# The second attention stage with the query blocks of its first batch rising and of its last batch falling, and the next batch's keys loaded in other pieces

## The chip, the cores and the metric

The kernel runs on one core of one Trainium2 chip. The metric is the device time of one execution in microseconds (us): 2022.06 before the change, the median of three runs (2018.59 to 2034.35). Lower is better.

## What is computed

Two layers work on `x`, four batches of 1024 tokens by 128 features. Each layer normalises the tokens, runs an attention and a mixture of experts on the result, and adds the product of the two (the experts' output behind a silu) to `x`. The change touches the attention of the second layer alone, which the reference writes as follows:

```
q = (xn @ Wq.T).reshape(B, S, 2 * H, hd).transpose(0, 2, 1, 3) * scaling
k, v = ...
scores = jnp.einsum('bhqd,bhkd->bhqk', q, k)
causal = jnp.triu(jnp.full((S, S), -jnp.inf), 1)
attn = jax.nn.softmax(scores + causal, axis=-1).reshape(B, H, 2, S, S)
w = attn[:, :, 0] - lam * attn[:, :, 1]
o = jnp.einsum('bhqk,bhkd->bhqd', w, v)
o = o * jax.lax.rsqrt(jnp.mean(o * o, axis=-1, keepdims=True) + EPS) * (1.0 - LAMBDA_INIT)
x = x + (o.transpose(0, 2, 1, 3).reshape(B, S, -1) @ Wo.T) * silu(experts(xn))
```

There are 16 score heads of 8 features. The mask is causal, so a block of 128 queries with number b (0 to 7 within its batch) needs only the key blocks 0 to b: b + 1 of them, 36 in a batch, 144 in the stage.

## The kernel before, in words

The program has four stages one behind the other: tokens of layer 0, attention of layer 0, the routed experts, and the attention of layer 1 (`attention_stage(1, ...)`), which is the last.

A unit u of the attention (0 to 31) is one block of 128 queries; units 0 to 7 are the first batch, 8 to 15 the second, and so on. `block_order` says which block a unit takes. Before, in the second layer, every batch goes 0, 7, 1, 6, 2, 5, 3, 4: a short unit and a long one alternate.

A unit goes through these steps. The names are those of the kernel's plan.

- `max`: TensorE makes the scores of the queries against the keys (`row_scores`, L1685, with the mask rows L1661 for the block on the diagonal), and VectorE reduces them to a row maximum (L2039). One reduction takes 1024 columns at most; the blocks 0 to 7 need 2, 4, 6, 10, 10, 12, 14 and 18 of them. Behind the last one of a unit VectorE splits the maxima into three bfloat16 parts (L2045 to L2054).
- `mrow`, `mcopy`, `msplit`: TensorE transposes the maxima (L1952), ScalarE copies them to SBUF (L1901), and a DMA on SP's queue (L1706) writes them as extra rows of the queries, `QS`.
- `exp`: for each key block TensorE makes the scores again, transposed and with the maxima taken off by those extra rows (`far_scores`, L1672), in two halves of 8 heads; ScalarE takes the exponential of each half (L1876). So a key block costs two exponentials of 128x1024.
- `av`: TensorE multiplies with the values (L1975), once for each key block, and gathers in one PSUM bank, `AV`.
- `ocopy`, `oback`, `onorm`: ScalarE copies that bank out (L1890), TensorE transposes it back (L1983), VectorE divides by the sums and prepares the norm (L2061 to L2084). Behind `ocopy` ScalarE also issues the loads of the next batch (below).
- Once for two units: `orms` on GpSimd (L1819 to L1822, the inverse square root), `oturn` and `oproj` on TensorE (L1990, L1995), with `oturned` on ScalarE between them (L1906), `final` on VectorE (L2109) and on GpSimd (L1836), and the store on SP's queue (L1743).
- Beside them the experts' outputs are fetched for two units: gathers on GpSimd (L1766) and a load of x on SP's queue (L1727), and `weigh` (ScalarE, L1855), `mix` (GpSimd, L1774), `tanh` (ScalarE, L1863), `gate` (GpSimd, L1780 and L1782).

Score tiles of `max` and `exp` share three PSUM slots of two banks. `mrow`, `oback`, `oturn` and `oproj` share one bank, `MISC`, which one user holds at a time.

The order on every engine is fixed before the run: `attention_plan` is a list scheduler that takes the steps of all units with costs (`COST`), with an aim for each kind of step in units of u (`AIM`: `max` of u near u - 0.9, `exp` near u + 1.3) and with their dependencies, and writes one list of steps for each engine. The engines run these lists in order and wait for each other through semaphores. In the plan the `mrow` of unit u stands behind the first `exp` of unit u - 2. Both the old and the new block order go through the same scheduler with the same costs and aims.

Keys and values of a batch lie in one of two buffers. The keys of the next batch come in six DMAs: two halves, each in the three runs of `KRUNS` (384, 256 and 128 KB); the values come in one DMA (544 KB in rows of 544 bytes). ScalarE issues them behind the `ocopy` of the units for which `feeds` is true: before, the first half of the keys in the first unit of a batch, the second half in the second, the values in the third (`load_piece`, L608 and L602).

## Time and profile before

| | |
|---|---|
| median of 3 runs | 2022.06 us (2018.59 to 2034.35) |
| the profiled execution | 2009.26 us, span 2007.4 us, so 1.9 us around it |
| mean granted TensorE clock | 0.889 of full speed |
| busy over the span | TensorE 81%, VectorE 66%, ScalarE 58%, GpSimd 55% |
| attention of layer 1 | from 1392.1 us to the end at 2007.4 us |

Times are us from the span's start. In a row of the timeline the first number is the start, the second the time from the start of the first to the end of the last of the merged instructions (xN says how many), then engine, line, operation and the tiles; the bracket says how long the engine had been idle and what ended that. SPq and ACTq are the queues on which SP and ScalarE issue DMAs; the time of a merged row there holds the waits between the issues. A window's row gives, for each engine, busy us and the count of instructions, then the granted clock (1.00 is 2.4 GHz, 0.50 is 1.2 GHz), the share of the DMA engines and GB/s.

### The profile page before, as it was taken

To read this page: it belongs to the slowest core of one execution; us is meant where nothing else is said; L and a number is where in the kernel's file an instruction comes from. 1 tells how busy PE (TensorE), PEld (TensorE's weight loads), DVE (VectorE), ACT (ScalarE), POOL (GpSimd) and SP (SyncE) were. 2 spreads that over 40 slices of the span, in tenths; PEclk is the share of its full clock that TensorE was granted. 3 is DMA by queue.
4 is the path that set the end of the run, shared out by engine and by line. 5 is a ranking of instruction groups with operands and counts; after the bars stand their busy time and mean duration, and the time that the engine had idled before them with its cause. 6 is when DMAs were issued, how large, how long until landed. Compare 5 with 4: busy or idle time off the path is not lost. (4 is left out here: it accounts for less than half of the span.)

```text
span 2007.4 us, 77167 instructions
## 1 busy us (share of the span) xinstructions
PE 1620.5 (81%) x33422; PEld 1255.6 (63%) x33422; DVE 1322.0 (66%) x1921; ACT 1171.6 (58%) x1500; POOL 1098.2 (55%) x1104
## 2 busy tenths in 40 slices
PE   6888789989999999999997633487778778778776
PEld 4666677777787777788785523376445545555554
DVE  5553767778777767768786342255877677677673
ACT  2333477777787777778785321154556556556555
POOL 4755488888899788978986265001222222222211
PEclk9888799999999999999998665698799799788788
DMA  3355023222332233322221172362121121111100
GB/s 96 97 172 141 24 90 92 75 82 77 103 99 55 82 94 97 86 65 66 74 70 56 57 215 82 100 176 75 40 51 29 44 50 28 49 47 27 30 13 10
DMA packets 189005, 151.47 MB, mean 75 GB/s; under 512 B 92163, under 2 KB 178190, under 8 KB 183166
## 3 DMA queue, kind: packets, MB, share of 16 engines
q1 hardware_dynamic: 161526, 103.80, 18.2%
q10 hardware_dynamic: 20088, 27.00, 4.3%
q0 software_dynamic: 7056, 15.74, 2.7%
q8 instruction: 267, 4.37, 0.9%
q14 instruction: 68, 0.56, 0.1%
HBM read 98.91 MB, written 46.79 MB: 73 GB/s over the span
## 5 line engine op out<-in xcount | busy, mean ns | idle before, releaser
L1876 ACT ACTIVATE a_EX<-bank 128x1024 f32<-128x1024 f32 x624 | 615.0, 1027 | 296.9 <-PE bank L1672 233.0
L2015 DVE TENSOR_TENSOR a_PM<-bank,a_PM 128x1024 f32<-128x1024 f32 x336 | 400.6, 1222 | 121.7 <-PE bank L1672 110.1
L1797 POOL TENSOR_TENSOR a_SN<-a_SN,a_MB 128x1024 f32<-128x1024 f32 x176 | 420.8, 2431 | 41.8 <-DMA a_MB<-m_dram 40.6
L2039 DVE TENSOR_REDUCE a_M<-bank 128x2 f32<-128x1024 f32 (+3 forms) x296 | 330.9, 1163 | 111.2 <-PE bank L1685 74.3
L1975 PE MATMUL bank<-a_EX,VV 128*32 128x128 f32 x9984 | 378.8, 294 | 11.1 <-issue 9.2
L1672 PE MATMUL bank<-QS,KS 51*128 51x128 bf16 (+1 forms) x4992 | 248.4, 233 | 95.0 <-DVE a_M L2039 33.0
L1975 PEld LDWEIGHTS bank<-a_EX,VV 128*32 128x32 f32 x9984 | 279.3, 117 | 62.7 <-issue 36.1
L1672 PEld LDWEIGHTS bank<-QS,KS 51*128 51x128 bf16 (+1 forms) x4992 | 163.9, 101 | 191.0 <-DVE a_M L2039 54.0
L1872 ACT ACTIVATE a_SN<-bank 128x1024 f32<-128x1024 f32 x176 | 176.8, 1024 | 61.0 <-PE bank L1651 59.3
L1651 PE MATMUL bank<-QP,rel_t 112*128 112x32 bf16 x5632 | 198.1, 177 | 3.7 <-issue 3.4
L1880 ACT ACTIVATE a_SN<-a_SN 128x1024 f32<-128x1024 f32 x176 | 184.3, 1058 | 22.8 <-POOL a_SN L1797 22.7
L1651 PEld LDWEIGHTS bank<-QP,rel_t 112*128 112x128 bf16 x5632 | 170.4, 96 | 4.7 <-issue 4.5
L1685 PE MATMUL bank<-KS,QS 48*128 48x128 bf16 (+3 forms) x1152 | 123.2, 302 | 41.6 <-DVE a_M L2039 16.7
L1766 POOL DMA_INDIRECT a_XG<-y_dram,KR x64 | 61.9, 967 | 155.8 <-DMA y_dram<-t_Y 130.0
L1672 PE MATMUL bank<-QS,KR 48*128 48x128 bf16 (+1 forms) x2688 | 123.9, 224 | 28.7 <-DVE a_PM L2015 12.8
L1646 PE MATMUL bank<-QN,KS 112*128 112x64 bf16 x2816 | 141.2, 193 | 7.2 <-PEq L710 5.7
L575 POOL COPY QP<-QS 48x1024 bf16<-48x1024 bf16 x64 | 137.4, 2148 | 0.0
L1672 PEld LDWEIGHTS bank<-QS,KR 48*128 48x128 bf16 (+1 forms) x2688 | 79.3, 97 | 73.9 <-DVE a_PM L2015 30.1
L2022 DVE TENSOR_TENSOR a_PM<-a_SN 128x1024 f32<-128x1024 f32 x64 | 97.9, 1530 | 31.6 <-ACT a_SN L1872 25.4
L1646 PEld LDWEIGHTS bank<-QN,KS 112*128 112x128 bf16 x2816 | 106.4, 98 | 12.5 <-issue 10.3
L1975 PE MATMUL bank<-a_SN,VV 128*32 128x128 f32 x2816 | 106.9, 291 | 4.3 <-ACT a_SN L1880 4.2
L1685 PEld LDWEIGHTS bank<-KS,QS 48*128 48x128 bf16 x1152 | 45.0, 100 | 98.6 <-issue 41.9
(213 smaller groups left out, 2286.5 us busy)
## 6 DMA issues: line engine op xcount, KB each, us to landing
a_MB<-m_dram SPq DMA_DIRECT2D x32, 1024.0 KB, 5.3
QS<-q_dram SPq DMA_DIRECT2D x192, 96.0 KB, 3.0
q_dram<-t_PARTS SPq DMA_DIRECT2D x32, 192.0 KB, 3.0
k_dram<-t_PARTS SPq DMA_DIRECT2D x16, 384.0 KB, 3.7
KS<-k_dram ACTq DMA_DIRECT2D x16, 384.0 KB
xs_dram<-bv SPq DMA_DIRECT2D x26, 192.0 KB, 4.8
t_XS<-xs_dram SPq DMA_DIRECT2D x18, 256.0 KB, 4.1
y_dram<-t_Y ACTq DMA_DIRECT2D x18, 256.0 KB, 2.3
```

What stands on the lines that cost most here:

```text
L575: last = pool.tensor_copy(QP[rows, r, :, :, a], QS[rows, q, :, :, :].rearrange("k p h (q b) -> k q (p h) b", b=2)[:, :, :, a])
L1646: pe.matmul(out_b[:, :, 4 * pair:4 * pair + 4], KS[0:KD, it.u // NB % 2, pair, it.jb * P:(it.jb + 1) * P], QN[:, r, pair, q0:q0 + CQ // 2, ...
L1651: last = pe.matmul(out_b[:, i, :], rel_t[:, y:y + P], QP[:, r, q0 + i, :, :].rearrange("k h a -> k (h a)"), start=False, stop=i == CQ // 2 ...
L1672: last = pe.matmul(bank[:, 2 * it.n + hh, k * P:(k + 1) * P], kblock(hh, rows, it.u, it.jb, pair), QS[hh * HALF:hh * HALF + rows, it.u % Q ...
L1685: last = pe.matmul(bank[:, 2 * it.n + hh, k * width:(k + 1) * width], QS[rows, it.u % QR, p0 + k, hh, :], KS[rows, it.u // NB % 2, p0 + k, ...
L1797: pool.tensor_tensor(near_view(sn), near_view(sn), as_near(MB[:, :, :], it.part), ALU.add)\
L1872: act.activation(near_buffer(u, jb)[:, part, :], src.rearrange("p b c -> p (b c)"), ACT.Copy).then_inc(act_done, 1)
L1876: act.activation(as_banks(EX[:, it.need % ER[layer]], part), by_head, ACT.Exp, scale=SCALE).then_inc(act_done, 1)
L1880: act.activation(sn, sn, ACT.Exp, scale=SCALE).then_inc(nexp_done, 1)
L1975: last = pe.matmul(dst_o, VV[:, u // NB % 2, jb, vo:vo + 32], ex, start=bool(it.first) and h < 4, stop=bool(it.last), skip_group_check=True)
L2015: dve.tensor_tensor(pm, mb.rearrange("p hh (k i) -> p hh k i", k=4), pm, ALU.max).then_inc(max_used, 1)
L2039: dve.tensor_reduce(target[:, :, p0:p0 + g], mb[:, :, 0:g * width].rearrange("p hh (k j) -> p hh k j", k=g), AX.X, ALU.max).then_inc(max_u ...
```

## The change

In the second layer the first batch takes its blocks in rising order (0, 1, ... 7) and the last batch in falling order (7, 6, ... 0); the two batches between stay as they were. The loads of the next batch are cut in another way: the first unit of a batch loads run 0 of both key halves (768 KB), the second run 1 of both (512 KB), the third run 2 of both (256 KB), the fourth the values. The first layer is the same as before.

```
-    return k if layer == 0 else (k // 2 if k % 2 == 0 else NB - 1 - k // 2)
+    if layer == 0 or u < NB:
+        return k
+    if u >= UNITS - NB:
+        return NB - 1 - k
+    return k // 2 if k % 2 == 0 else NB - 1 - k // 2
...
 def feeds(layer, u):
-    return u % NB < (5, 3)[layer] and u // NB + 1 < B
+    return u % NB < (5, 4)[layer] and u // NB + 1 < B
...
+        def load_keys(eng, b, k, run, to=KS, src=k_dram):
+            s0, parts = run
+            row = k % 2 * HALF + s0 * DH
+            eng.dma_start(to[row:row + parts * DH, b % 2, :, :].rearrange("r p t -> r (p t)"),
+                          src[b][0:parts, k % 2].rearrange("s d p t -> s d (p t)")).then_inc(kv_in[b % 2], 16)
...
                             if feeds(layer, u):
-                                load_piece(layer, act, u // NB + 1, u % NB)
+                                if layer == 0:
+                                    load_piece(layer, act, u // NB + 1, u % NB)
+                                elif u % NB == len(KRUNS):
+                                    load_piece(layer, act, u // NB + 1, 2)
+                                else:
+                                    for k in range(2):
+                                        load_keys(act, u // NB + 1, k, KRUNS[u % NB])
```

The scheduler makes new lists from this. On ScalarE, the beginning of the stage stood like this before (`a_MP` is `mcopy`, `a_XG` is `weigh`, `a_TH` is `tanh`, `a_EX` is `exp`, `OS` is `ocopy`):

```order
L1901 ACTIVATE a_MP<-bank 48x128
L1855 ACTIVATE a_XG<-a_XG,KR 128x128 x4
L1863 ACTIVATE a_TH<-a_XG 128x256
L1855 ACTIVATE a_XG<-a_XG,KR 128x128 x4
L1863 ACTIVATE a_TH<-a_XG 128x256
L1855 ACTIVATE a_XG<-a_XG,KR 128x128 x4
L1876 ACT_TABLE_LOAD
L1876 ACTIVATE a_EX<-bank 128x2x4x128
L1863 ACTIVATE a_TH<-a_XG 128x256
L1901 ACTIVATE a_MP<-bank 48x128
L1876 ACTIVATE a_EX<-bank 128x2x4x128
L1890 ACTIVATE OS<-bank 128x512
```

In the changed kernel (its lines stand 8 further down, and 14 behind the loads) the same beginning is:

```order
L1915 ACTIVATE a_MP<-bank 48x128
L1863 ACTIVATE a_XG<-a_XG,KR 128x128 x4
L1915 ACTIVATE a_MP<-bank 48x128
L1884 ACT_TABLE_LOAD
L1884 ACTIVATE a_EX<-bank 128x2x4x128 x2
L1871 ACTIVATE a_TH<-a_XG 128x256
L1863 ACTIVATE a_XG<-a_XG,KR 128x128 x4
L1898 ACTIVATE OS<-bank 128x512
L606 DMA KS<-k_dram 24x1x8192 x2
L1871 ACTIVATE a_TH<-a_XG 128x256
L1884 ACTIVATE a_EX<-bank 128x2x4x128 x2
L1863 ACTIVATE a_XG<-a_XG,KR 128x128 x4
```

The exponentials of unit 0 now stand ahead of the first `tanh`, and the `tanh` of the later pairs stand between the exponentials of units 1 and 2.

On TensorE the end of the program stood like this before (`OS` is `oback`, `a_OF` is `oturn`, `wo,a_OT` is `oproj`, `a_EX,VV` is `av`, `QS,KS` is `exp`):

```order
L1672 MATMUL bank<-QS,KS 128x128 x16
L1990 MATMUL bank<-eye,a_OF 128x128 x2
L1975 MATMUL bank<-a_EX,VV 32x128 x16
L1995 MATMUL bank<-wo,a_OT 128x128 x2
L1672 MATMUL bank<-QS,KS 128x128 x16
L1661 MATMUL bank<-mask_b 128x4x64 x4
L1983 MATMUL bank<-eye,OS 128x128 x4
L1672 MATMUL bank<-QS,KS 128x128 x8
L1661 MATMUL bank<-mask_b 128x4x64 x4
L1975 MATMUL bank<-a_EX,VV 32x128 x64
L1983 MATMUL bank<-eye,OS 128x128 x4
L1990 MATMUL bank<-eye,a_OF 128x128 x2
```

In the changed kernel the last rows are:

```order
L1680 MATMUL bank<-QS,KS 128x128 x8
L1669 MATMUL bank<-mask_b 128x4x64 x4
L1989 MATMUL bank<-a_EX,VV 32x128 x32
L1997 MATMUL bank<-eye,OS 128x128 x4
L1989 MATMUL bank<-a_EX,VV 32x128 x48
L2004 MATMUL bank<-eye,a_OF 128x128 x2
L2009 MATMUL bank<-wo,a_OT 128x128 x2
L1997 MATMUL bank<-eye,OS 128x128 x8
L2004 MATMUL bank<-eye,a_OF 128x128 x2
L2009 MATMUL bank<-wo,a_OT 128x128 x2
```

The last score matmuls, which stood between the `oturn` of units 28 and 29 and the `oback` of units 30 and 31, now stand ahead of all of them: `oback` of unit 29, `oturn` and `oproj` of units 28 and 29, and `oback` of units 30 and 31 follow each other with no score between.

## Rows read from the trace of the kernel before

**Rows 1.** Windows: us, busy us of each engine (instructions), granted clock, DMA share, GB/s
```profile
core 0: us, PE busy (x) PEld busy (x) DVE busy (x) ACT busy (x) POOL busy (x), PEclk, DMA share, GB/s
1560.00:1710.00 150.00, 118.78 (x2216) 77.12 (x2212) 108.09 (x168) 84.83 (x113) 41.59 (x92) 0.86 0.16 42
...
1420.00:1500.00 80.00, 65.48 (x1271) 42.91 (x1273) 62.55 (x92) 47.56 (x63) 17.58 (x43) 0.87 0.19 49
```

**Rows 2.** Waits of TensorE from 1560 to 1860: who for whom, us, times, longest
```profile
PE bank L1672 <- DVE a_M L2039: 16.1, 23, 2.2
PE bank L1952 <- DVEq L2055: 8.0, 7, 2.0
PE bank L1685 <- DVE a_M L2039: 6.5, 5, 2.3
```

**Rows 3.** Timeline of ScalarE: first exponential of units 9 and 25
```profile
1573.67 2.16 ACT L1876 ACTIVATE a_EX<-bank 128x1024 f32<-128x1024 f32 x2 [2.46 <-PE bank L1672]
...
1874.93 1.02 ACT L1876 ACTIVATE a_EX<-bank 128x1024 f32<-128x1024 f32 x1 [2.39 <-PE bank L1672]
```

**Rows 4.** Timeline of ScalarE from 1971 to 1990: the last 17 exponentials
```profile
1971.83 2.85 ACT L1876 ACTIVATE a_EX<-bank 128x1024 f32<-128x1024 f32 x3 [0.17 <-PE bank L1672]
...
1975.03 7.48 ACT L1876 ACTIVATE a_EX<-bank 128x1024 f32<-128x1024 f32 x8
...
1982.74 1.18 ACT L1876 ACTIVATE a_EX<-bank 128x1024 f32<-128x1024 f32 x1
...
1984.82 4.68 ACT L1876 ACTIVATE a_EX<-bank 128x1024 f32<-128x1024 f32 x5
```

**Rows 5.** Timeline of VectorE: behind the last reduction of units 1 and 9
```profile
1418.65 0.20 DVE L2045 TENSOR_REDUCE a_MT<-a_M 128x16 f32<-128x48 f32 x1
...
1559.59 0.20 DVE L2045 TENSOR_REDUCE a_MT<-a_M 128x16 f32<-128x48 f32 x1
```

**Rows 6.** Timeline of SP's queue at the start of the stage
```profile
1392.09 14.77 SPq L1727 DMA_DIRECT2D a_XG<-x_mid  x8
1406.91 15.55 SPq L1706 DMA_DIRECT2D QS<-a_MP  x4
```

**Rows 7.** The page's DMA issues: KB each, us to landing
```profile
QS<-q_dram SPq DMA_DIRECT2D x192, 96.0 KB, 3.0
```

**Rows 8.** Timeline of ScalarE at the start: table load and first exponential
```profile
1414.71 1.28 ACT L1876 ACT_TABLE_LOAD   x1
1418.83 1.02 ACT L1876 ACTIVATE a_EX<-bank 128x1024 f32<-128x1024 f32 x1 [2.83 <-issue]
```

**Rows 9.** Timeline of ScalarE at the start: the first two `tanh`
```profile
1403.53 0.42 ACT L1863 ACTIVATE a_TH<-a_XG 128x256 f32<-128x256 f32 x1 [1.69 <-issue]
...
1409.43 0.42 ACT L1863 ACTIVATE a_TH<-a_XG 128x256 f32<-128x256 f32 x1 [3.77 <-POOL a_XG L1774]
```

**Rows 10.** Timeline of TensorE, VectorE and GpSimd at the end
```profile
1984.10 0.41 PE L1990 MATMUL bank<-eye,a_OF 128*128 128x128 f32 x2 [1.14 <-POOL a_OF L1822]
...
1986.86 0.66 PE L1983 MATMUL bank<-eye,OS 128*128 128x128 f32 x4
...
1992.51 0.63 PE L1983 MATMUL bank<-eye,OS 128*128 128x128 f32 x4 [0.81 <-ACT OS L1890]
...
1993.17 0.26 DVE L2061 RECIPROCAL a_RC<-bank 128x16 f32<-128x16 f32 x1 [3.42 <-PE bank L1983]
...
1995.47 0.20 POOL L1819 TENSOR_SCALAR a_SS<-a_SS 128x16 f32<-128x16 f32 x1 [8.00 <-DVEq L2085]
...
2001.29 0.66 PE L1990 MATMUL bank<-eye,a_OF 128*128 128x128 f32 x2 [8.15 <-POOL a_OF L1822]
```

**Rows 11.** Windows with loads of the next batch (first row) and without (second)
```profile
1574.00:1614.00 40.00, 33.32 (x600) 21.87 (x602) 27.28 (x43) 22.66 (x30) 12.22 (x32) 0.83 0.23 58
...
1875.00:1915.00 40.00, 33.24 (x606) 21.65 (x606) 28.19 (x43) 22.93 (x31) 12.58 (x33) 0.84 0.10 26
```

**Rows 12.** The page's 40 slices: GB/s of each
```profile
GB/s 96 97 172 141 24 90 92 75 82 77 103 99 55 82 94 97 86 65 66 74 70 56 57 215 82 100 176 75 40 51 29 44 50 28 49 47 27 30 13 10
```

More of the change, by code:

```diff
@@ L605, in load_piece @@
                 to, src = (KS, k_dram) if k < 2 else (KR, kr_dram)
-                for s0, parts in KRUNS:
-                    row = k % 2 * HALF + s0 * DH
-                    eng.dma_start(to[row:row + parts * DH, b % 2, :, :].rearrange("r p t -> r (p t)"),
-                                  src[b][0:parts, k % 2].rearrange("s d p t -> s d (p t)")).then_inc(kv_in[b % 2], 16)
+                for run in KRUNS:
+                    load_keys(eng, b, k, run, to, src)
         def token_stage(x_src, stage):
```

## The prediction

> **What bounds the kernel now.** I read the windows first. In the steady middle of the second attention stage no engine is full: in the 150 us from 1560 TensorE is busy 118.8, VectorE 108.1, ScalarE 84.8, at a mean clock of 0.86 [rows 1]. So the table of waits comes next: over two batches (300 us) TensorE waits 16.1 + 8.0 + 6.5 = 30.6 us for VectorE's reductions and splits, 15.3 a batch [rows 2], and the rest of its idle time is small gaps between steps. The reader is to see a coupled pipeline: `max` and `exp` share TensorE and three PSUM slots, and each runs slower for the other. Third, the timeline at the two ends, where one of the two streams runs alone.
>
> Three prices follow. **Mixed**: from the first exponential of unit 9 to that of unit 25 two batches pass, 1874.93 - 1573.67 = 301.3 us [rows 3] for 72 key blocks, 4.18 us for one `max` block and one `exp` block together, everything included. **`exp` alone**: the last 17 exponentials run with no `max` beside them, from 1971.83 to 1984.82 + 4.68 = 1989.50, 17.67 us [rows 4], 1.04 each and 2.08 a block. **The share of `max` in the mix** is what is left, 4.18 - 2.08 = 2.10. I treat the mix as additive (so much for each `max` block, so much for each `exp` block); that is the choice on which the sum stands, and the rivals are what happens if it fails.
>
> **The start.** Before, VectorE goes through unit 0 and all 18 reductions of unit 1 (9 blocks), to 1418.65 [rows 5], before the first exponential at 1418.83 [rows 8]. After, unit 1 has two blocks, and by the order on ScalarE the table load and the first exponentials stand behind one `weigh` only. What is late next is SP's queue: eight loads of x stand ahead of the first row of maxima, one behind the other, until 1406.91 [rows 6], and they stay there. The first row then needs its landing; the trace gives none for it, so I take the 3.0 us of the query loads on the same queue [rows 7], which gives 1409.9. The score and mask matmuls and the table load of 1.28 [rows 8], partly beside each other, put the first exponential at an estimated 1412.5, 6.3 us sooner. By then TensorE has issued, in its list, 8 reductions: units 0 and 1 and a third of unit 2, 4 blocks instead of 9, since the remaining ones of unit 2 stand behind the first `exp`. Five more `max` blocks are left for the mix: 5 x 2.10 = 10.5. Net: -6.3 + 10.5 = **+4.2 us**.
>
> The `tanh` of pairs 3, 5 and 7, which lay beside `max` of unit 1, now stand between the exponentials of units 1 and 2. In the trace one `tanh` follows the other by 1409.43 - 1403.53 = 5.9 us [rows 9], because `mix` and `gate` on GpSimd and two gathers lie between them. From 1414.6, behind the first two exponentials, three such steps end at 1432.3, and 0.4 later unit 2's exponentials may start. By the mix, 6 `max` blocks and 3 `exp` blocks from 1412.5 end at 1412.5 + 12.6 + 6.2 = 1431.3. So the chain costs **+1.4 us**; the bounds are 0 and, if all of it stood alone, 1432.7 - 1412.5 - 6.2 = 14.
>
> **The end.** By TensorE's list 20 `exp` steps (10 blocks) stood behind the last `max` step before, and 10 (5 blocks) stand there after. That is no gain by itself: by the additive mix the 5 blocks cost 2.08 each either way. What changes is the tail behind the last exponential. Before: 2007.4 - 1989.50 = 17.9 us. After, the order on TensorE sets a chain with nothing beside it. From the `oback` of unit 29: to the start of `orms` 1995.47 - 1992.51 = 2.96; to `oturn` 2001.29 - 1995.47 = 5.82; `oturn` to the next `oback` 1986.86 - 1984.10 = 2.76; then `oback` and `onorm` of unit 30 and `onorm` of unit 31 (they share VectorE and `MISC`), 2.96 + (1995.47 - 1993.17) = 5.26; `orms` again 5.82; and from `oturn` to the end 2007.4 - 2001.29 = 6.11 [rows 10]. Together 28.7. The `ocopy` ahead of it ends one exponential (1.0) before the last exponential does and hands over in 0.15, so the tail is 28.7 + 0.15 - 1.0 = 27.9 us: **+10.0 us**. Before, the first three of these steps lay beside exponentials of unit 31.
>
> In the falling batch, from unit 26 on, fewer `max` blocks than `exp` blocks run together, so TensorE waits less for VectorE. Of the 15.3 us a batch [rows 2] I take half, **-7.7 us**; the bounds are 0 and all 15.3. In the rising batch I take no such gain, since there the `max` blocks are the larger part. Check: VectorE needs 108.1 / 36 = 3.0 us a block [rows 1], 96 us for the 32 blocks left at 1413; the mix for them and the 21 `exp` blocks of units 0 to 5 is 32 x 2.10 + 21 x 2.08 = 111, so the mix is the larger and stands.
>
> **The loads** stay seven issues and the same bytes for a batch, at the same engine; they are done long before the next batch. A stretch with them and the same stretch of the last batch without them hold the same work: TensorE 33.3 and 33.2 us busy, VectorE 27.3 and 28.2 in 40 us, though the DMA share is 0.23 against 0.10 [rows 11]. I cost them at 0. If the cover went, the small row of maxima would wait for the load issued before it: at the best slice of the page, 215 GB/s [rows 12], 768, 512 and 256 KB in the short units of the start take 3.6 + 2.4 + 1.2 = 7.2 us. The Trainium skill speaks against the change here: "Trainium Kernel Development and Optimization", Key Constraints, says that DMAs issued from the SP, ACT and POOL queues all run on the same 16 engines and interleave. By that rule the sum would be up to those 7.2 us higher; rows 11 don't show it in the middle of the stage, and no row shows it for units as short as those at the start.
>
> **The sum.** 4.2 + 1.4 + 10.0 - 7.7 = +7.9 us. Against the profiled execution: 2009.26 (span 2007.4 and 1.9 around it) becomes 2017.2. That execution lies 12.8 us below the median of the runs and below all three of them, so I carry the difference to the median: 2022.06 + 7.9 = 2030.0 us, 0.4% more. A measurement of this kernel can tell about 1%, 20 us, from no change; the forecast is that it can't be told.
>
> **Rivals.**
>
> *The orders without short-long meetings run better than the mix (faster).* For it: TensorE is busy only 118.8 of 150 us, and 15.3 of the idle time are waits for VectorE. Then VectorE runs the rising batch full: its 32 blocks end at 1413 + 96 = 1509; the 7 `exp` blocks of unit 6 alone take 14 x 1.04 = 14.6; unit 7's 8 beside unit 9 at TensorE's busy time of 118.8 / 36 = 3.3 take 26.4; and with 1573.67 - 1559.59 = 14.1 from the split of unit 9's maxima to its first exponential, as before [rows 3, 5], this comes at 1564.1 instead of 1573.67, -9.6. In the falling batch all 15.3 go, and the tail stays at +10.0: -9.6 - 15.3 + 10.0 = -14.9, which is 2007. The mean clock of 0.86 means that TensorE spends 0.28 of a batch, 42 us, at 1.2 GHz, which would be 21 at 2.4; if the two new batches together won half of one batch's 21, another 10 us would go: 1997. Against it: VectorE has drains and waits for its slots even at the start, when it had nothing else to do.
>
> *VectorE starves in the rising batch (slower).* The place is units 3 to 7, where each `max` step shares three slots with an `exp` step, in a list made by aims that fit the old order. For it: in 1420 to 1500, with the same long units, VectorE is busy 62.55 of 80 us, 78% [rows 1]. At that pace 96 us become 123, `max` of unit 7 ends at 1536, and the first exponential of unit 9 comes at 1536 + 14.6 + 26.4 + 14.1 = 1591, +17.4 instead of +5.6. With no relief in the falling batch and the tail of +10.0: +27.4, 2050. It decides against the forecast once VectorE's busy share there is under 87%.
>
> *The loads collide with the rows of maxima.* +7.2 on the forecast: 2037.
>
> **How the numbers follow.** The forecast has 0.50, the faster rival 0.19, the slower one 0.24, the colliding loads 0.07. The faster rival reaches 20 us only with the clock's help, so 0.11 of it counts as faster by over 1% and 0.08 as within; of the slower one 0.21 is over 1%, and of the forecast and the loads, whose unknown costs spread by some 12 us, 0.09 is over 1% too. That makes faster 0.11, within 1% 0.59, slower 0.30. The range for 8 in 10 goes from 2004, between the faster rival's two ends, to 2053, just past the slower one.
>
> **What would show it.** In the trace after: first exponential near 1412.5 and the loads of x still ahead of the first `msplit`; `tanh` between the exponentials of units 1 and 2, about 6 us apart; VectorE's busy share between 1420 and 1510 (above 87% for the forecast); the first exponential of unit 9 near 1579; the tail from the last exponential near 28 us, with `oturn` of units 28 and 29 waiting for GpSimd. A tail near 18, or unit 9 before 1565, would make the prediction wrong on the fast side; unit 9 after 1590 on the slow side.

## The result, and the profile after

| | before | after |
|---|---|---|
| median (20 runs each) | 2021.85 us (2008.99 to 2034.35) | 2036.96 us (2025.89 to 2047.75) |
| ratio, 95% interval | | 1.0074 (1.0054 to 1.0094) |
| profiled execution, span | 2009.26, 2007.4 | 2036.38, 2034.5 |

The change costs 0.74%, about 15 us. The forecast was 2030.0, within 1%, with a range of 2004 to 2053: the time fell into it, 7 us above the forecast. That a change of this size can't be told from none did not hold: with 20 runs on each side the interval lies clear of 1. The page after begins so:

```profile
span 2034.5 us, 77167 instructions
...
PE 1630.5 (80%) x33422; PEld 1260.9 (62%) x33422; DVE 1314.8 (65%) x1921; ACT 1172.4 (58%) x1500; POOL 1108.3 (54%) x1104
```

The two spans differ by 27.1 us, but not all of that is the change. VectorE's first reduction of the stage, in the timeline before and then after:

```profile
1392.97 2.36 DVE L2039 TENSOR_REDUCE a_MT<-bank 128x8 f32<-128x1024 f32 x2 [1.71 <-PE bank L1661]
```
```profile
1405.72 2.36 DVE L2053 TENSOR_REDUCE a_MT<-bank 128x8 f32<-128x1024 f32 x2 [1.67 <-PE bank L1669]
```

12.7 us lie ahead of the stage, in work that the change doesn't touch. So every profile is read from that reduction on. In ScalarE's timeline after, the first exponentials of units 0, 9, 17 and 21 and the last one of all are:

```profile
1425.17 1.94 ACT L1884 ACTIVATE a_EX<-bank 128x1024 f32<-128x1024 f32 x2
...
1604.02 2.16 ACT L1884 ACTIVATE a_EX<-bank 128x1024 f32<-128x1024 f32 x2 [2.50 <-PE bank L1680]
...
1750.49 2.16 ACT L1884 ACTIVATE a_EX<-bank 128x1024 f32<-128x1024 f32 x2 [2.54 <-PE bank L1680]
...
1828.28 2.15 ACT L1884 ACTIVATE a_EX<-bank 128x1024 f32<-128x1024 f32 x2 [1.16 <-PE bank L1680]
...
2004.78 1.03 ACT L1884 ACTIVATE a_EX<-bank 128x1024 f32<-128x1024 f32 x1
```

Before, units 17 and 21 began here (units 0 and 9 are in [rows 3, 8], the last exponential in [rows 4]):

```profile
1723.67 4.20 ACT L1876 ACTIVATE a_EX<-bank 128x1024 f32<-128x1024 f32 x4 [2.52 <-PE bank L1672]
...
1804.61 2.15 ACT L1876 ACTIVATE a_EX<-bank 128x1024 f32<-128x1024 f32 x2 [1.06 <-PE bank L1672]
```

These cut the stage into four pieces. "First exp" is from the first reduction to the first exponential, "start" from the first reduction to unit 9, "middle" from unit 9 to unit 21, "falling" from there to the end of the last exponential, "tail" the rest. The same for every experiment, in us; each ratio is to the kernel before as it ran beside that experiment, so the time that it stands beside below is not always the same:

| kernel | ratio to before (95%) | first exp | start | middle | falling | tail | stage |
|---|---|---|---|---|---|---|---|
| before | 1 | 25.9 | 180.7 | 230.9 | 184.9 | 17.9 | 614.4 |
| after | 1.0074 (1.0054 to 1.0094) | 19.5 | 198.3 | 224.3 | 177.5 | 28.7 | 628.8 |
| e2_loads | 0.9952 (0.9929 to 0.9975) | 27.0 | 179.0 | 229.2 | 183.8 | 18.0 | 610.0 |
| e3_rise | 1.0091 (1.0054 to 1.0128) | 19.8 | 200.9 | 230.7 | 182.3 | 18.0 | 631.9 |
| e4_fall | 1.0044 (1.0018 to 1.0070) | 26.8 | 182.2 | 232.5 | 178.9 | 28.6 | 622.2 |
| e5_late | 1.0043 (1.0015 to 1.0070) | 19.5 | 190.8 | 225.0 | 174.5 | 28.6 | 618.9 |
| e6_list | 0.9949 (0.9924 to 0.9974) | 24.3 | 175.2 | 224.1 | 181.7 | 18.0 | 599.0 |
| e7_tail | 1.0069 (1.0039 to 1.0099) | 18.6 | 196.4 | 225.1 | 176.8 | 21.0 | 619.3 |
| e8_chain | 1.0120 (1.0101 to 1.0139) | 18.0 | 206.6 | 224.9 | 174.2 | 28.6 | 634.3 |
| e10_chain2 | 1.0075 (1.0049 to 1.0100) | 19.5 | 202.2 | 224.6 | 175.4 | 28.7 | 630.9 |
| e9_best | 0.9933 (0.9912 to 0.9955) | 24.9 | 173.9 | 223.7 | 173.5 | 21.0 | 592.1 |
| e11_split | 1.0085 (1.0054 to 1.0115) | 18.3 | 207.5 | 222.3 | 176.6 | 28.6 | 635.0 |
| e12_bestsplit | 0.9920 (0.9890 to 0.9950) | 23.7 | 175.1 | 224.0 | 176.8 | 20.9 | 596.8 |

The pieces come from one profile each and scatter by some us: the falling parts of kernels with the same falling order lie between 173.5 and 178.9, the starts with the old first batch between 173.9 and 182.2 (in part another list, as the experiments show). The ratios come from many runs.

After against before: +17.6 in the start, -6.6 in the middle, -7.4 in the falling batch, +10.8 in the tail, together +14.4 us, which is what the medians show (15.1). The forecast had +5.6, 0, -7.7 and +10.0.

**The start.** ScalarE's timeline after, from the first exponential of unit 0 to the first of unit 2 (ACTq rows are its DMA issues):

```profile
1423.51 0.27 ACT L1915 ACTIVATE a_MP<-bank 48x128 bf16<-48x128 f32 x1 [8.91 <-PE bank L1966]
...
1442.99 1.92 ACT L1884 ACTIVATE a_EX<-bank 128x1024 f32<-128x1024 f32 x2
...
1448.15 0.60 ACT L1898 ACTIVATE OS<-bank 128x512 f32<-128x512 f32 x1 [0.17 <-issue]
1448.17 1.46 ACTq L606 DMA_DIRECT2D KS<-k_dram  x2
...
1459.62 1.94 ACT L1884 ACTIVATE a_EX<-bank 128x1024 f32<-128x1024 f32 x2 [7.42 <-PE bank L1680]
```

and TensorE's at the same place:

```profile
1450.47 0.61 PE L1693 MATMUL bank<-KS,QS 48*128 48x512 bf16 x2
...
1458.97 1.04 PE L1680 MATMUL bank<-QS,KS 51*128 51x128 bf16 x16 [7.89 <-DMA QS<-a_MP]
```

TensorE stands 7.89 us in front of unit 2's scores, and what ended the wait is the row of maxima of unit 2. It goes out on SP's queue in two DMAs, at 1448.04 and 1448.83, beside the 512 KB that ScalarE put on its own queue from 1448.17 on. The view of the DMA queues from 1448 to 1462 shows these loads (the GB/s are of 40 slices of 0.35 us):

```profile
GB/s 0 0 0 0 18 94 6 0 47 47 47 47 0 47 47 94 48 48 48 48 48 48 50 47 95 48 48 48 48 47 47 94 47 47 47 47 0 0 0 0
...
KS<-k_dram ACTq DMA_DIRECT2D x2, 256.0 KB
QS<-a_MP SPq DMA_DIRECT2D x2, 6.0 KB
```

The two key loads run at some 47 GB/s, not at the 215 of [rows 12], and last from 1449.9 to 1461.0. By the trace's DMA records they go in 32 packets of 16 KB, never more than two at a time, 0.61 us each (median). The row of maxima was issued by 1449.56 and landed at 1458.84, 9.3 us later; rows that meet no load land 1.24 us behind their issue. The records show the waiting packet by packet: the first of the row's two DMAs was through by 1449.56, ahead of the first key packet; of the second one's 24 packets of 256 bytes eight went at once, from 1450.23 to 1450.35, and the other sixteen one by one from 1453.93 to 1457.93, with 16 KB key packets between them. That is the colliding rival of the prediction, in unit 2 instead of spread over three units. By the Trainium skill, "Trainium Kernel Development and Optimization", Key Constraints, DMAs of the SP, ACT and POOL queues share the same 16 engines and interleave; the 9.3 us against 1.24 agree with it, and [rows 11], on which I had set it aside, did not hold for the start.

The waits of TensorE from unit 0's first exponential to unit 9's, after:

```profile
PE bank L1680 <- ACT a_EX L1884: 9.6, 12, 3.8
PE bank L1693 <- ACT a_EX L1884: 8.3, 14, 2.4
PE bank L1680 <- DVE a_M L2053: 8.2, 10, 2.5
PE bank L1680 <- DMA QS<-a_MP: 7.9, 1, 7.9
```

and before (1420 to 1573):

```profile
PE bank L1672 <- ACT a_EX L1876: 3.1, 6, 0.7
...
PE bank L1685 <- ACT a_EX L1876: 2.0, 5, 0.6
```

Beside the new wait for the DMA, TensorE waits 17.9 us for slots that exponentials hold, instead of 5.1. VectorE's busy share in the `max` work of the first batch is 91.91 / 121.20 = 76% (from the windows after), against 78.90 / 106.00 = 74% before:

```profile
1425.20:1546.40 121.20, 83.34 (x1307) 50.05 (x1305) 91.91 (x126) 54.62 (x80) 34.70 (x63) 0.77 0.15 40
```
```profile
1418.80:1524.80 106.00, 85.36 (x1608) 56.04 (x1610) 78.90 (x118) 62.29 (x83) 24.05 (x51) 0.85 0.17 43
```

So VectorE, which has more of its work in this stretch, is as little full as before. The granted clock is lower in this stretch, 0.77 against 0.85, but that is not where the time goes. From the first reduction to unit 9, where TensorE does the same work in both kernels, the windows before and after are:

```profile
1392.97:1573.67 180.70, 135.64 (x2405) 84.08 (x2400) 139.36 (x207) 94.42 (x134) 56.30 (x103) 0.81 0.17 44
```
```profile
1405.72:1604.02 198.30, 133.98 (x2404) 83.82 (x2398) 141.38 (x207) 93.89 (x133) 56.65 (x103) 0.81 0.15 40
```

The clock is 0.81 in both, TensorE is busy 135.6 and 134.0 us, and what grows is its idle time, from 45.1 to 64.3 us.

**The tail.** TensorE at the end, after:

```profile
2005.03 0.63 PE L1997 MATMUL bank<-eye,OS 128*128 128x128 f32 x4 [0.91 <-ACT OS L1898]
...
2013.83 0.66 PE L2004 MATMUL bank<-eye,a_OF 128*128 128x128 f32 x2 [4.40 <-POOL a_OF L1830]
...
2016.70 1.12 PE L1997 MATMUL bank<-eye,OS 128*128 128x128 f32 x4 [0.52 <-DVE a_XO L2123]
...
2018.99 1.11 PE L1997 MATMUL bank<-eye,OS 128*128 128x128 f32 x4 [1.17 <-DVE a_ON L2087]
...
2028.30 0.66 PE L2004 MATMUL bank<-eye,a_OF 128*128 128x128 f32 x2 [8.19 <-POOL a_OF L1830]
```

This is the chain that the prediction wrote down: `oback` of unit 29, `oturn` of units 28 and 29 waiting for GpSimd, `oback` of units 30 and 31, and `oturn` again behind 8.19 us of GpSimd. From the end of the last exponential, 2004.78 + 1.03 = 2005.81, to 2034.5 it takes 28.7 us.

**The falling batch.** From unit 21 to the last exponential TensorE waited 21.1 us for VectorE before (1804.61 to 1989.51) and 15.5 us after (1828.28 to 2005.81).

### The profile page after: what moved, and what is told of

It is laid out like the page before. It is cut to its first block and busy times, and to the rows that moved or that the text cites. A ratio compares the mean times of both kernels' runs of the same rounds, so it can differ in the third digit from the quotient of the medians.

```text
span 2034.5 us, 77167 instructions
## 1 busy us (share of the span) xinstructions
PE 1630.5 (80%) x33422; PEld 1260.9 (62%) x33422; DVE 1314.8 (65%) x1921; ACT 1172.4 (58%) x1500; POOL 1108.3 (54%) x1104
## 5 line engine op out<-in xcount | busy, mean ns | idle before, releaser
L1888 ACT ACTIVATE a_SN<-a_SN 128x1024 f32<-128x1024 f32 x176 | 184.6, 1058 | 27.3 <-POOL a_SN L1805 27.1
```

The source lines that it names most:

```text
L1888: act.activation(sn, sn, ACT.Exp, scale=SCALE).then_inc(nexp_done, 1)
```

## The experiments

**One part alone.** The first three take the change apart.

e2_loads keeps the old order of blocks and takes only the new cut of the loads, with the new `feeds`:

```
-    if layer == 0 or u < NB:
-        return k
-    if u >= UNITS - NB:
-        return NB - 1 - k
-    return k // 2 if k % 2 == 0 else NB - 1 - k // 2
+    return k if layer == 0 else (k // 2 if k % 2 == 0 else NB - 1 - k // 2)
```

> Only the new cut of the loads; block order as before. Theory A (the cut matters only where a row of maxima is needed at once): start 181, the two middle batches as before, 150 us each, the whole within 0.3% of before. Rival (the new cut is what made the middle of the changed kernel 6.6 us shorter): from the first exponential of unit 9 to that of unit 21 about 224 us (before 231), the whole 0.3% below before.

Measured: 2017.01 us beside 2023.06, 0.9952 (0.9929 to 0.9975). The part that I had costed at 0 makes the kernel 0.5% faster.

e3_rise takes only the rising first batch, with the loads and `feeds` of before:

```
     if layer == 0 or u < NB:
         return k
-    if u >= UNITS - NB:
-        return NB - 1 - k
     return k // 2 if k % 2 == 0 else NB - 1 - k // 2
```

> Only the rising first batch; last batch and loads as before. Theory A (two separate losses, about 17 us at the start and about 3 us at the end): start near 198 (the old loads are in flight behind units 0 and 1 too), from the first exponential of unit 21 to the end as before, 203 us, tail behind the last exponential 18; the whole 0.8% above before. Rival (the old cut of the loads is harmless and the new one made the loss): start below 192, the whole within 0.5% of before.

Measured: 2041.13 beside 2023.06, 1.0091 (1.0054 to 1.0128); start 200.9. The row of its waits (TensorE) shows that the old cut collides too, and no less:

```profile
PE bank L1678 <- DMA QS<-a_MP: 9.6, 1, 9.6
```

e4_fall takes only the falling last batch:

```
-    if layer == 0 or u < NB:
+    if layer == 0:
         return k
```

> Only the falling last batch; first batch and loads as before. Theory A: start 181 as before; from the first exponential of unit 21 to the last exponential about 177 (before 185), tail behind the last exponential about 28 (before 18): +3 us, the whole 0.15% above before. Rival (falling order itself runs worse): 185 or more to the last exponential, the whole 0.5% above.

Measured: 2031.51 beside 2023.06, 1.0044 (1.0018 to 1.0070): tail 28.6, falling part 178.9 instead of 184.9.

The three ratios add to 0.91 + 0.44 - 0.48 = 0.87%, where the change measures 0.74%: within the intervals, the parts add. The rising batch carries most of the loss, and the falling one alone is a loss too: its part gets 6.0 us shorter and its tail 10.7 us longer.

**The collision.** e5_late is the changed kernel with the loads of the second batch's keys, in the cut of before, all behind the fourth unit's `ocopy`, ahead of the values:

```
                                 elif u % NB == len(KRUNS):
+                                    if u < NB:
+                                        for k in range(2):
+                                            load_piece(layer, act, 1, k)
                                     load_piece(layer, act, u // NB + 1, 2)
-                                else:
+                                elif u >= NB:
```

> The changed kernel, but in the first batch all loads of the next batch's keys and values are issued behind the ocopy of unit 3 instead of behind those of units 0 to 3. Measures: start = from VectorE's first reduction of the stage to the first exponential of unit 9 (before 180.7 us, changed 198.3). Theory A (the start loses about 8 us because the rows of maxima of unit 2 land behind the key loads): they land about 1.2 us after their issue, TensorE's wait of 7.9 us for them goes, start about 190, the whole 0.4% above before. Theory B (VectorE starves in the rising batch because max and exp share slots, the loads don't matter): start stays near 198, the whole 0.7% above.

Measured: 2033.75 beside 2023.06, 1.0043 (1.0015 to 1.0070). From the first reduction to unit 9 it takes 1602.59 - 1411.81 = 190.8 us instead of 198.3:

```profile
1411.81 2.36 DVE L2056 TENSOR_REDUCE a_MT<-bank 128x8 f32<-128x1024 f32 x2 [1.67 <-PE bank L1669]
...
1602.59 4.20 ACT L1884 ACTIVATE a_EX<-bank 128x1024 f32<-128x1024 f32 x4 [2.50 <-PE bank L1680]
```

Some 7.5 us of the start are the collision, about the 7.89 us of the wait itself. The loads now delay the row of unit 5 (it lands 15.3 us behind its issue), and TensorE doesn't wait for that one. VectorE's busy share in the first batch rises from 76% to 91.55 / 113.70 = 81%:

```profile
1431.30:1545.00 113.70, 82.95 (x1307) 49.20 (x1305) 91.55 (x126) 54.51 (x80) 34.56 (x63) 0.78 0.17 42
```

The other 10.1 us (190.8 - 180.7) are idle time of TensorE, at a clock of 0.82 where it was 0.81 before. The whole start, and TensorE's waits for ScalarE in it from 1431 to 1602:

```profile
1411.81:1602.59 190.78, 133.48 (x2405) 82.88 (x2398) 140.99 (x207) 93.72 (x133) 56.46 (x103) 0.82 0.16 42
```
```profile
PE bank L1680 <- ACT a_EX L1884: 8.1, 11, 2.9
...
PE bank L1693 <- ACT a_EX L1884: 6.4, 12, 1.1
PE bank L2000 <- ACT OS L1898: 4.6, 3, 4.2
...
PE bank L2000 <- ACT a_MP L1918: 2.1, 1, 2.1
```

TensorE idles 57.3 us here and 45.1 before. It waits 14.5 us for slots that exponentials hold (5.1 before, from 1420 to 1573) and 6.7 us in front of `oback` for ScalarE's copies (0.2 before); for VectorE it waits 18.7 us (16.1 before). So most of the new waiting is for ScalarE, which is itself busy for only 93.7 of the 190.8 us. Which of its steps come late, and why, no run shows.

**Where the middle's gain comes from.** The blocks of the second and third batch stand as before, and yet the middle is 6.6 us shorter. Either the new cut of the loads does it, or the list: `feeds` is also what tells the scheduler that a fourth unit's `ocopy` has loads behind it, and with that it plans another order. I had written that both orders go through the scheduler with the same costs; they do not. e6_list is the kernel before with that entry alone; its loads stay as they were:

```
-    return u % NB < (5, 3)[layer] and u // NB + 1 < B
+    return u % NB < (5, 4)[layer] and u // NB + 1 < B
...
-                            if feeds(layer, u):
+                            if feeds(layer, u) and (layer == 0 or u % NB < 3):
```

> Block order and loads of before; only the scheduler is told that four units of a batch issue loads, so that it makes the list of the middle batches that the changed kernel has. Theory A (the middle of the changed kernel is shorter because of this other list): from the first exponential of unit 9 to that of unit 21 about 226 us (before 231), the whole 0.3 to 0.5% below before, as with the new cut of the loads. Theory B (it is the cut of the DMAs that does it): 231 us there, the whole as before.

Measured: 2003.24 beside 2014.77, 0.9949 (0.9924 to 0.9974), as much as e2_loads. The first reduction, and the first exponentials of units 9, 17 and 21:

```profile
1400.29 2.36 DVE L2039 TENSOR_REDUCE a_MT<-bank 128x8 f32<-128x1024 f32 x2 [1.67 <-PE bank L1661]
...
1575.47 4.20 ACT L1876 ACTIVATE a_EX<-bank 128x1024 f32<-128x1024 f32 x4 [2.39 <-PE bank L1672]
...
1721.97 4.20 ACT L1876 ACTIVATE a_EX<-bank 128x1024 f32<-128x1024 f32 x4 [2.46 <-PE bank L1672]
...
1799.58 1.02 ACT L1876 ACTIVATE a_EX<-bank 128x1024 f32<-128x1024 f32 x1 [1.16 <-PE bank L1672]
```

The middle takes 1799.58 - 1575.47 = 224.1 us, as in the changed kernel (224.3). All kernels with the new entry lie at 222.3 to 225.1 there but e2_loads (229.2); all with the old one at 230.8 to 232.5. TensorE's list between units 9 and 21 is the same in all of the first and differs from the old in some 40 of its 322 places. In e2_loads, which has the same list, the middle is long because TensorE ran slower there, not because it waited; the windows from unit 9 to unit 21 before, in e6_list and in e2_loads:

```profile
1573.67:1804.61 230.94, 184.84 (x3427) 120.28 (x3427) 166.13 (x255) 131.01 (x173) 64.75 (x148) 0.86 0.17 43
```
```profile
1575.47:1799.58 224.11, 182.43 (x3423) 117.70 (x3424) 165.42 (x255) 131.42 (x173) 64.99 (x148) 0.88 0.17 45
```
```profile
1590.10:1819.29 229.19, 189.13 (x3423) 122.02 (x3424) 165.88 (x255) 131.44 (x172) 64.84 (x148) 0.84 0.17 44
```

TensorE's idle time is 46.1 us with the old list and 41.7 and 40.1 with the new one; in e2_loads a granted clock of 0.84 and 189.1 us of work hide the gain. So the gain is the scheduler's new order, not the loads. The middle is not all of the 0.5%: where the first batch keeps its old order, the new entry changes 32 of TensorE's 240 steps ahead of unit 9 too (with the rising batch it changes none), and the start is 173.9 to 179.0 us with the new list, 180.7 and 182.2 with the old one. Of that, TensorE's idle time went from 45.1 and 45.3 us to between 41.2 and 43.3; the rest went with the granted clock, 0.81 to 0.86 in these starts.

**The tail.** e7_tail is the changed kernel in which `oturn`, `oproj` and `final` of units 28 and 29 stand behind `oback` and `onorm` of units 30 and 31, so that GpSimd's second `orms` starts before that work:

```
+    move("pe", (("oturn", end - 2), ("oproj", end - 2)), ("oback", end))
+    move("act", (("oturned", end - 2),), ("ocopy", end))
+    move("dve", (("final", end - 2),), ("onorm", end))
+    move("pool", (("final", end - 2),), ("orms", end))
...
+                            pool.wait_ge(ot_psum, units_before + u // span)
```

> The changed kernel with the last pair's oback and onorm of units 30 and 31 ahead of oturn, oproj and final of units 28 and 29 (and orms of the last pair ahead of GpSimd's final of the pair before). Theory A (the longer tail is the chain that oturn of units 28 and 29 puts ahead of oback 30): from the last exponential to the end 21 to 22 us instead of 28.7, the whole about 7 us below the changed kernel. Rival (the tail is long because the units are short, whatever the order): 27 us or more.

Measured: the last exponential ends at 1992.28 + 1.03 = 1993.31 and the span at 2014.3, a tail of 21.0 us instead of 28.7:

```profile
1992.28 1.03 ACT L1901 ACTIVATE a_EX<-bank 128x1024 f32<-128x1024 f32 x1
...
1996.86 0.66 PE L2014 MATMUL bank<-eye,OS 128*128 128x128 f32 x4
...
1998.68 0.66 PE L2014 MATMUL bank<-eye,OS 128*128 128x128 f32 x4 [1.16 <-DVE a_ON L2104]
...
2001.46 0.41 PE L2021 MATMUL bank<-eye,a_OF 128*128 128x128 f32 x2 [2.12 <-POOL a_OF L1847]
...
2008.13 0.66 PE L2021 MATMUL bank<-eye,a_OF 128*128 128x128 f32 x2 [4.58 <-POOL a_OF L1847]
```

The two `oback` (1996.86 and 1998.68) now stand ahead of both `oturn`, and the second `oturn` comes 6.67 us behind the first instead of 14.47. The time as a whole, 1.0069 (1.0039 to 1.0099), does not show these 7.7 us: they would be 0.4%, and the interval is as wide.

**The `tanh` chain.** Beyond the collision the start is still 190.8 - 180.7 = 10.1 us longer. Two runs ask whether the `tanh` and `weigh` steps between the first exponentials are the cause, both on top of e5_late. e8_chain moves them on ScalarE behind exponentials and `ocopy` of units 1 and 2:

```
+    slots = {("ocopy", 1, None, None): ("tanh1", "weigh3"), ("exp", 2, 0, 1): ("tanh3", "weigh5"),
+             ("exp", 2, 1, 1): ("tanh5", "weigh7"), ("ocopy", 2, None, None): ("tanh7",)}
```

> The kernel with the late loads (start 190.8 us to the first exponential of unit 9), with ScalarE's tanh of pairs 1 to 7 and weigh of pairs 3 to 7 moved behind the exponentials of unit 1. Theory A (the chain tanh, gate, mix between the exponentials of units 1 and 2 costs some 6 us of the rest of the start): unit 2's first exponential at 40 us instead of 45, start 185 or 186. Rival (the rest of the start is the max blocks that now share TensorE with exp): start 189 or more.

Measured: 2038.87 beside 2014.77, 1.0120 (1.0101 to 1.0139); start 206.6. Slower, although the first exponentials of units 1 and 2 come sooner (27.6 and 41.2 us after the first reduction, 29.6 and 45.3 in e5_late); it is lost behind them, by unit 3 it is 70.7 against 60.7. Over the whole start TensorE idles 61.7 us, 4.4 more than in e5_late, and is busy 145.0 instead of 133.5, at a granted clock of 0.76 instead of 0.82: most of the loss is TensorE at a lower clock. e10_chain2 moves the whole chain, GpSimd's part too, among the exponentials of units 3 and 4:

```
+    moved("act", ("weigh3", "tanh3", "weigh5", "tanh5", "weigh7", "tanh7"),
+          {("exp", 3, 0, 1): ("weigh3",), ("exp", 3, 1, 1): ("tanh3", "weigh5"), ("exp", 3, 2, 1): ("tanh5", "weigh7"),
+           ("exp", 3, 3, 1): ("tanh7",)})
+    moved("act", ("weigh9", "tanh9"), {("exp", 4, 0, 1): ("weigh9",), ("exp", 4, 2, 1): ("tanh9",)})
+    moved("pool", ("mix3", "gate3", "mix5", "gate5", "mix7", "gate7"),
+          {("fetch", 9, None, None): ("mix3", "gate3", "mix5", "gate5", "mix7", "gate7")})
```

> As the run before with the chain moved, but now the whole chain goes: weigh, mix, tanh and gate of pairs 3, 5 and 7 stand beside the exponentials of unit 3 on ScalarE, and on GpSimd behind orms, final and the next fetches of pair 1, so that neither the exponentials of units 1 and 2 nor oturn of the first pair wait for them. Loads late. Theory A (the chain is what is left of the start's loss beyond the 4 us of moved max blocks): unit 2's first exponential near 40 us (45 with the late loads alone), unit 3's near 55 (61), start 185 or 186. Rival (max and exp sharing TensorE make it): start 189 or more.

Measured: 2036.27 beside 2021.36, 1.0075 (1.0049 to 1.0100). The first exponentials of units 1, 2 and 3 come 30.1, 44.8 and 60.2 us after the first reduction, where e5_late has 29.6, 45.3 and 60.7: at the same time, with none of the chain of pairs 3, 5 and 7 between them. That does not agree with e8_chain, where unit 2 came 4.1 us sooner; and in e10_chain2 ScalarE idles 1.82 us between the exponentials of unit 1 in a wait that the profile marks as remote, without a step that ended it. Later units lose (unit 9 at 202.2), here too at a lower clock: 0.78 over the start, TensorE busy 143.3 us and idle 58.9. Neither run makes the start or TensorE's idle time shorter, both run it at a lower clock, and so what the chain costs, and what makes up the other 10 us, stays open.

**How the loads are cut.** The rest is about the collision: is it the small number of packets at a time? By the Trainium skill, "DMA: Bandwidth & Descriptors", section "Why a DMA increments its semaphore by 16 and not by 1", such a DMA runs on the largest number of engines up to 16 that divides the slowest dimension that is not 1 of both sides, here 3, 2 and 8 for the pieces (the last has a single part of 8 rows). The trace agrees as far as it goes, with at most three packets at a time in the 768 KB of unit 0, two in the 512 KB of unit 1 and eight in the 256 KB of unit 2. Those eight already told something: they took 0.93 to 2.10 us each instead of 0.61, and the 256 KB took 3.5 us, 76 GB/s. e11_split is the changed kernel with one DMA for each part of 8 rows, and TensorE's count of them set to match:

```
+            if split:
+                for s in range(parts):
+                    eng.dma_start(to[row + s * DH:row + (s + 1) * DH, b % 2, :, :].rearrange("r p t -> r (p t)"),
+                                  src[b][s, k % 2].rearrange("d p t -> d (p t)")).then_inc(kv_in[b % 2], 16)
+                return
```

> The changed kernel with each key load of the next batch issued part by part (8 rows of 16 KB each: 12 DMAs for a batch instead of 6, the same bytes, units and engine). Theory: a key load moves few packets at a time (in the changed kernel never more than two in the 512 KB piece, 0.61 us each), and the row of maxima behind it waits for those. Parts of 8 rows should move up to 8 packets at a time; then 32 packets take about 32 / 8 x 0.61 = 2.4 us, the row of maxima of unit 2 lands 1.2 to 3.5 us behind its issue instead of 9.3, TensorE's wait of 7.9 us for it goes to under 2, and the first exponential of unit 9 comes 189 to 193 us after the stage's first reduction (198.3 as changed, 190.8 with the loads moved away). [...] Rival: the bytes themselves are what holds the row up, however they are cut; then it lands more than 6 us late again and unit 9 stays near 198. A price on both: ScalarE issues four more DMAs behind unit 0's ocopy and two more behind unit 1's, 0.73 us each, up to 3 us. Ratio to the kernel before: 1.003 to 1.006 by the theory, 1.007 to 1.009 by the rival.

Measured: 2034.12 beside 2015.11, 1.0085 (1.0054 to 1.0115). My theory fell. Up to nine packets are on the way at once, but each takes 1.81 us (median) instead of 0.61, and the 512 KB take 7.7 us instead of 11.0. The row of unit 2 lands 8.65 us behind its issue, just behind the last key packet, and TensorE's wait is the same:

```profile
PE bank L1685 <- DMA QS<-a_MP: 7.8, 1, 7.8
```

Now gathers are held up too. `weigh` in front of unit 1's second pair of exponentials waits for one:

```profile
1441.70 1.27 ACT L1868 ACTIVATE a_XG<-a_XG,KR 128x128 f32<-128x128 f32 x4 [5.96 <-DMA a_XG<-y_dram,KR]
```

In the changed kernel that wait was 1.06 us. So in both cuts the row waits for key packets, which is the rival's side; but the rival had unit 9 near 198, and it comes at 207.5. Of these 9.2 us more, 3.3 are idle time of TensorE and 5.9 are busy time, at a granted clock of 0.77 instead of 0.81. What bounds these loads at 47 to 76 GB/s stays open.

**The version that beats both.** e9_best takes the parts that gain: the old order in the first batch, the falling last batch, the new loads and list, and the tail of e7_tail:

```
-    if layer == 0 or u < NB:
+    if layer == 0:
         return k
...
+    move("pe", (("oturn", end - 2), ("oproj", end - 2)), ("oback", end))
...
```

> The first batch as before, the last batch falling, the new cut of the loads and the shorter tail of the run before. If the parts add up: e2's gain (0.5%) and the falling batch's gain of some 6 us, less 4 us for a tail of 22 us instead of 18: 2010 to 2014 us, ratio 0.994. Rival (the parts don't add): 0.999 or more.

Measured: 2001.12 beside 2014.77, 0.9933 (0.9912 to 0.9955), faster than the kernel before and the changed one. That it is faster than the new list alone is not shown: e6_list has 0.9949 (0.9924 to 0.9974), and the two intervals overlap. e12_bestsplit is the same with the split of e11_split:

> The kernel that beat both (first batch in the old order, last one falling, the new loads, the reordered tail) with the key loads part by part as in the run beside it. In its trace the rows of maxima of units 4, 10, 12, 18 and 20 landed 5.7 to 7.2 us behind their issue and TensorE did not wait for them. By the theory that these were hidden, they land within 3.5 us now and the time does not move: ratio to the kernel before 0.991 to 0.996. Rival: late rows cost something in the middle too, some 1 to 2 us each through the order of what follows; then the ratio is 0.988 to 0.990 and unit 9 to unit 21 takes under 220 us instead of 223.7.

Measured: 1997.09 beside 2015.11, 0.9920 (0.9890 to 0.9950), not to be told from e9_best. The rows of maxima landed 3.8 to 8.4 us behind their issue, so the split didn't clear them, and the run can't say whether late rows cost anything in the middle.

## Why the prediction was right, and where its steps were not

The time fell into the range and into the likeliest case, within 1%. The steps one by one:

- **First exponential 6.3 us sooner.** Measured 25.9 - 19.5 = 6.4. The number held, its reason not. I had it wait for the row's landing behind SP's loads of x, at 3.0 us [rows 7]. The row of unit 0 landed 1.24 us behind its issue, at 1421.7; the exponential waited on ScalarE behind unit 1's `mcopy` (1423.51, 8.91 us for TensorE) and the table load.
- **Five `max` blocks more in the mix, net +4.2, and the `tanh` chain, +1.4.** Together +5.6; measured +17.6. The largest miss. 7.5 of the 12 us too little are the loads (next point). What the `tanh` chain costs is not settled, e8_chain and e10_chain2 disagree on it. About 4.5 us (190.8 - 180.7 - 5.6) are left, and the step that they belong to is the additive mix with 2.10 us for a `max` block: in the rising batch it cost more. The price came from a stretch in which TensorE waits for VectorE [rows 2]; in e5_late's start it waits 14.5 us for slots that exponentials hold, and 6.7 us for ScalarE's copies, 21.2 us where it was 5.3 before. VectorE is at 81% there. Why ScalarE's steps come late was not settled.
- **The loads at 0.** This step failed: [rows 11] compare stretches in the middle, where rows of maxima have time to spare, and say nothing of units of one to three blocks. e5_late gives +7.5. The colliding rival had 7.2, but by the wrong working: at 215 GB/s, and summed over three units. It is one wait in one unit, behind 512 KB at 47 GB/s.
- **The middle at 0.** Not a term of the prediction at all, and worth -6.6. I took `feeds` as a matter of loads; it is also an entry in the scheduler's costs, and its new list is what e6_list shows to be 0.5% faster with nothing else changed, though part of that is in the start.
- **The falling batch, -7.7.** Measured -7.4 in the changed kernel and -6.0 in e4_fall. TensorE's waits for VectorE there fell by 5.6 us (21.1 to 15.5), so the reason holds in the main. The half of [rows 2] was taken without working, between bounds of 0 and 15.3; that it came so near is luck.
- **The tail, +10.0.** Measured 28.7 - 17.9 = +10.8. The chain is the one written down, step by step, and e7_tail confirms it from the other side: taking the first `oturn` and its `oproj` out of the chain gives 7.7 us back.

The sum was +7.9 and the stage shows +14.4. Two things left out, +7.5 from the loads and -6.6 from the list, nearly cancel; that the forecast is only 7 us off is luck to that extent.

The rivals: the faster one fell, since VectorE never came near full in the rising batch. The slower one had unit 9 at +17.4 with VectorE under 87%; measured +17.6 at 76%. Its sign was right, and the slots that exponentials hold, which it named, cost TensorE 9.4 us more in e5_late than before. But nearly half of its price at the start is the DMA collision, which it did not name, and its other part, no relief in the falling batch, did not come.

## What to carry to other kernels

A small transfer on which an engine waits must not be issued right beside large loads, even when these are on another engine's queue; look at the shortest unit that the loads run beside, not at the mean of a busy stretch. When a table of costs or flags feeds a scheduler, an edit to it moves work far from the edited place: compare the lists everywhere before costing the rest at nothing. An order that ends on its shortest work shortens the mixed part but bares the chain behind the last step, so write that chain out and move whatever can go behind its longest wait.

## What the runs showed of the hardware that was not expected

- Key loads in rows of 16 KB run at 47 GB/s (512 KB in 11.0 us, two packets of 0.61 us at a time) where other slices of the page reach 215. With eight or nine packets at a time each takes 1.81 us, and the load still takes 7.7 us, 68 GB/s.
- A DMA of 6 KB on another queue, issued beside such loads, lands 8.65 to 9.3 us behind its issue instead of 1.24, its packets of 256 bytes standing between packets of 16 KB; in the kernel before, the rows of units 4, 10, 12, 18 and 20 landed 6.6 to 8.7 us behind their issue as well, and nothing waited for them.
